# Output projection with the first norm, and experts with the second norm, each as one stage worked tile by tile; rank matmuls 256 columns wide

## The reference, cut to what matters

```
o   = y @ out_proj.T                     # 1024 x 1024 by 1024 x 512
x   = x + layernorm(o)
h   = layernorm(x)
low = h @ A.T ; g = gates(h @ W_gate.T, h @ W_thr)      # 8 experts of rank 16
o   = h @ W_base.T + b_base + (2 * low * g) @ B
x   = x + layernorm(o)
h   = rmsnorm(layernorm(x)) * norm_w     # goes into layer 1
```

## Time and profile before

| | us |
|---|---|
| median of 3 runs | 2665.6 |
| lowest, highest | 2663.9, 2677.38 |
| span of the profiled execution | 2670.2 |
| TensorE busy in it | 2308.2 (86%) |
| VectorE busy | 1957.9 (73%) |
| ScalarE busy | 1460.8 (55%) |
| GpSimd busy | 1238.2 (46%) |

### The profile page before, as it was taken

How to read it: one execution, slowest core, us unless ns; L and a number is a source line. 1 busy time by engine, 2 the same in 40 slices (tenths; PEclk the granted TensorE clock), 3 DMA queues, 4 the chain that set the end, 5 groups by cost and what they waited for, 6 DMA issues and landing times. The chain is left out here.

```text
span 2670.2 us, 33973 instructions
## 1 busy us (share of the span) xinstructions
PE 2308.2 (86%) x11172; PEld 1672.4 (63%) x11172; DVE 1957.9 (73%) x3153; ACT 1460.8 (55%) x3092; POOL 1238.2 (46%) x788
## 2 busy tenths in 40 slices
PE   5966676667454999999999999999999999779997
PEld 4532222225434677777777777777777777569996
DVE  4559989994554786686685776775866866688777
ACT  2344444443103796685785866866956857742221
POOL 2119988993101464363462553644643624542212
PEclk9989998998576999999999999999999999899999
DMA  2030030000112232231332322322312312211010
GB/s 80 26 115 13 0 126 0 0 0 32 60 36 74 90 119 66 76 115 52 90 99 57 101 76 71 111 72 74 108 67 77 113 52 88 91 45 37 36 48 32
DMA packets 113218, 175.20 MB, mean 66 GB/s; under 512 B 9696, under 2 KB 77664, under 8 KB 112032
## 3 DMA queue, kind: packets, MB, share of 16 engines
q1 hardware_dynamic: 113056, 173.16, 20.6%
HBM read 166.71 MB, written 6.42 MB: 65 GB/s over the span
## 5 line engine op out<-in xcount | busy, mean ns | idle before, releaser
L78 PE MATMUL mg_pb<-xTh,mg_wh 128*128 128x512 f32 x1152 | 479.2, 416 | 16.9 <-POOL mg_wl L1233 16.9
L1243 POOL TENSOR_TENSOR mg_y<-mg_hT,mg_sg 128x512 f32<-128x512 f32 x128 | 187.7, 1466 | 598.9 <-DVE mg_hT L1479 598.9
L79 PE MATMUL mg_pb<-xTl,mg_wh 128*128 128x512 f32 x1152 | 454.3, 394 | 0.0
L80 PE MATMUL mg_pb<-xTh,mg_wl 128*128 128x512 f32 x1152 | 452.1, 392 | 0.0
L775 PE MATMUL ss_y<-ss_pr,cst 128*128 128x512 f32 x512 | 278.5, 678 | 125.7 <-POOL ss_pr L757 125.4
L1427 DVE SCALAR_TENSOR_TENSOR mg_hT<-mg_pb,mg_cw,mg_hT 128x510 f32<-128x510 f32 (+2 forms) x432 | 318.4, 741 | 31.6 <-ACT mg_hT L1599 22.8
L757 POOL TENSOR_TENSOR ss_pr<-o,ss_bc 128x1024 f32<-128x1024 f32 x128 | 301.9, 2374 | 45.9 <-DVE o L726 26.9
L1454 DVE TENSOR_TENSOR mg_m<-mg_gb,mg_cb 128x384 f32<-128x384 f32 x512 | 265.3, 549 | 71.6 <-ACT mg_gb L1649 68.2
L775 PEld LDWEIGHTS ss_y<-ss_pr,cst 128*128 128x128 f32 x512 | 98.4, 210 | 305.6 <-POOL ss_pr L757 225.8
L657 ACT ACTIVATE ss_da<-dt,ss_na 128x510 f32 (+1 forms) x256 | 165.9, 680 | 208.0 <-DVE o L726 208.0
L78 PEld LDWEIGHTS mg_pb<-xTh,mg_wh 128*128 128x128 f32 x1152 | 217.2, 189 | 76.5 <-issue 19.2
(11 more groups left out here) (289 smaller groups left out, 5217.4 us busy)
## 6 DMA issues: line engine op xcount, KB each, us to landing
mg_abc<-acs_rows SPq DMA_DIRECT2D x256, 256.0 KB, 3.4
mg_ws<-in_w_in SPq DMA_DIRECT2D x72, 512.0 KB, 3.8
ss_bc<-bc_rows SPq DMA_DIRECT2D x16, 1024.0 KB, 6.4
mg_wos<-in_w_out SPq DMA_DIRECT2D x64, 256.0 KB, 3.6
ff_ws<-in_w SPq DMA_DIRECT2D x7, 1024.0 KB, 4.7
x<-in_x SPq DMA_DIRECT2D x16, 256.0 KB, 4.1
ip_ws<-in_w_in SPq DMA_DIRECT2D x8, 512.0 KB, 3.6
ff_w2s<-in_w SPq DMA_DIRECT2D x7, 512.0 KB, 5.7
```

Source lines behind the costliest of these rows:

```text
L78: pe.matmul(out, lhs[0], rhs[0], start=start, stop=False)
L79: pe.matmul(out, lhs[0], rhs[1], start=False, stop=False)
L80: return pe.matmul(out, lhs[1], rhs[0], start=False, stop=stop)
L1243: pool.tensor_tensor(yb[:, p % RING, t], hT[s % 2][:, t], sg[s % 2][:, t], ALU.mult).then_inc(s_y2, 1)
```

## The change

Both norm stages are taken apart. The first norm of all (`first_norm`) keeps its operations. `out_proj_and_norm` takes the place of `scan_out_proj` and the n1 norm, `experts_and_norm` that of `experts` and the n2 norm. The 1024 channels' weights come in four transfers of two k-tiles into two buffers; x and the expert weights are loaded behind the first two. The projection runs tiles 0 to 3 with k outermost in four pairs of k, and tiles 4 to 7 one by one. As soon as a tile is done, its statistics, norm, addition and second norm follow per tile; GpSimd adds x, ScalarE norms o straight from its bank. In the experts stage the split of the weights is made at its start by ScalarE, VectorE and GpSimd; the rank matmuls read 256 columns (the last 118 of the base weights and the 138), of which the last 138 are used; the second scaling uses the variance instead of a sum of squares (var * r * r), norm_w is multiplied in by GpSimd before the transposition, and x_kept is written by tile. Semaphores of finished stages are cleared by SyncE and used again.

```diff
+def out_proj_and_norm(nc, sem, clear_stages, spare, sb, banks, I, xc, sz, o, x, xT, ex_ws, cst, eps, x_tok):
...
+            def _(sp):
+                for j in range(HT):
+                    if j >= 2:
+                        sp.wait_ge(s_wl, j - 1)
+                    sp.dma_start(ws[j % 2][:], I["w_out0"][:, 2 * j:2 * j + 2, :]).then_inc(s_w[j % 2], 16)
+                    if j == 1:
+                        for m in range(MT):
+                            sp.dma_start(x[:, m, :], x_tok[:, m, :]).then_inc(s_x, 16)
+                        sp.dma_start(ex_ws[:], I["w_ex"]).then_inc(s_x, 16)
+                cleared.extend(clear_stages(sp, "ip_", "sp_", "ss_", "n0_", "norm_"))
+                sp.wait_ge(s_x, 16 * (MT + 1))
...
+                def low(j):
+                    pool.wait_ge(s_hi, j + 1)
+                    wait_buffer(pool, j)
+                    pool.tensor_tensor(held(yl[j % 2], j), part(xc, j), held(yh[j % 2], j).bitcast(F32), ALU.subtract
+                                       ).then_inc(s_lop, 1)
+
+                def add_x(m):
+                    pool.wait_ge(s_n1, m + 1)
+                    pool.tensor_tensor(x[:, m, :], x[:, m, :], o[:, m, :], ALU.add).then_inc(s_x2, 1)
+
+                for j in range(HT):
+                    weights_low(j)
+                low(4)
+                pool.wait_ge(s_x, 16 * (MT + 1))
+                low(5)
+                for m in range(MT):
+                    add_x(m)
+                    if m < 2:
+                        low(6 + m)
...
+                for j in range(HT):
+                    pair(j)
+                tile(4)
+                tile(5)
+                turn(0)
+                turn(1)
+                tile(6)
+                turn(2)
+                turn(3)
+                tile(7)
+                for m in range(4, MT):
+                    turn(m)
...
+                high(4)
                 for m in range(MT):
...
+                    root(0, m)
+                    if m >= 1:
+                        root(1, m - 1)
+                    norm_o(m)
+                    if m < 3:
+                        high(5 + m)
+                    if m >= 2:
+                        x_high(m - 2)
...
+                for m in range(MT):
+                    stats_o(m)
+                    if m >= 1:
+                        stats_x(m - 1)
+                    invert_o(m)
+                    if m < 2:
+                        gated(6 + m)
+                    if m >= 1:
+                        normed(m - 1)
+                    if m >= 2:
+                        x_low(m - 2)
...
+def experts_and_norm(nc, sem, clear_stages, spare, sb, banks, I, xT, x, o, ex_ws, st_w, cst, eps, x_dram):
...
+                for m in range(MT):
+                    add_x(m)
+                    if m >= 1:
+                        weighted(m - 1)
+                weighted(MT - 1)
...
+                def rank(m):
+                    if m >= 2:
+                        pe.wait_ge(s_g, m - 1)
+                    t = slice(m * P, (m + 1) * P)
+                    for k in range(KD):
+                        i = mm3(pe, pk[m % 2][:, 0:RW], (xT[0][:, k, t], xT[1][:, k, t]),
+                                (wh[:, k, DM + N2 - RW:], wl[:, k, DM + N2 - RW:]), k == 0, k == KD - 1)
+                    i.then_inc(s_p, 1)
...
+                pe.wait_ge(s_wlv, 2)
+                pe.wait_ge(s_wlp, 2)
+                for m in range(MT):
+                    rank(m)
                 for m in range(4):
...
+                    base(m)
+                pe.wait_ge(s_b, 64)
+                turn_hw(0)
                 for m in range(MT):
...
+                    if m + 1 < MT:
+                        turn_hw(m + 1)
+                    up(m)
+                    if m + 4 < MT:
+                        base(m + 4)
+                    if m >= 3:
+                        turn(m - 3)
+                for m in range(MT - 3, MT):
+                    turn(m)
...
+                for k in range(KD):
+                    act.activation(wh[:, k, :], ex_ws[:, k, :], ACT.Copy).then_inc(s_wh, 1)
...
+                for m in range(MT + 3):
+                    if m < MT:
+                        copied(m)
+                        root(0, mv[0][:, m, 1:2], m)
+                    if 1 <= m <= MT:
+                        root(1, mv[1][:, m - 1, 1:2], m - 1)
+                    if m < MT:
+                        norm_o(m)
+                    if 1 <= m <= MT:
+                        root(2, ms[:, m - 1:m], m - 1)
+                    if 2 <= m <= MT + 1:
+                        scaled(m - 2)
+                    if m >= 3:
+                        x_high(m - 3)
...
+                for m in range(MT + 3):
+                    if m < MT:
+                        biased(m)
+                    if 1 <= m <= MT:
+                        stats_x(m - 1)
+                    if m < MT:
+                        invert_o(m)
+                    if 1 <= m <= MT:
+                        normed(m - 1)
+                        second(m - 1)
+                    if m >= 3:
+                        x_low(m - 3)
...
             @block.tensor
             def _(pe):
-                pe.wait_ge(s_lo, 2 * KD)
                 for h in range(NH):
```

More of the change, by code:

```diff
@@ new lines, in tile, with turn @@
+                def tile(m):
+                    pe.wait_ge(s_lop, m - HT + 1)
+                    if m >= 6:
+                        pe.wait_ge(s_n1, m - 5)
+                    hi, lo = held(yh[m % 2], m), held(yl[m % 2], m)
+                    for k in range(CD):
+                        last = mm3(pe, bank(m)[:], (hi[:, k, :], lo[:, k, :]), (wh[:, k, :], wl[:, k, :]),
+                                   k == 0, k == CD - 1)
+                    last.then_inc(s_out, 1)
+                def turn(m):
+                    pe.wait_ge(s_h, m + 1)
+                    if m >= 2:
+                        pe.wait_ge(s_xlo, m - 1)
+                    for k in range(KD):
+                        last = pe.transpose(tb[m % 2][:, k * P:(k + 1) * P], o[:, m, k * P:(k + 1) * P], ident)
+                    last.then_inc(s_t, 1)
@@ L853, in experts, with gated, low @@
-def experts(nc, sem, sb, banks, I, xT, o, ident, weights):
+                ch = Chain(dve, s_ch)
+                def gated(j):
+                    dve.wait_ge(s_sz, j + 1)
+                    dve.tensor_tensor(part(xc, j), part(xc, j), part(sz, j), ALU.mult).then_inc(s_y, 1)
+                def low(j):
+                    dve.wait_ge(s_hi, j + 1)
+                    wait_buffer(dve, j)
+                    dve.tensor_tensor(held(yl[j % 2], j), part(xc, j), held(yh[j % 2], j).bitcast(F32), ALU.subtract
+                                      ).then_inc(s_lo, 1)
@@ new lines, in _ @@
+                gated(0)
+                gated(1)
+                for j in range(HT):
+                    low(j)
+                    gated(j + 2)
+                for m in range(MT):
+                    stats_o(m)
[8 more added lines that the diff above has]
+                        x_low(m - 2)
@@ new lines, in _ @@
+                for m in range(MT):
+                    copied(m)
+                gates()
+                dve.wait_ge(s_b, 64)
+                for m in range(MT + 3):
[10 more added lines that the diff above has]
+                        x_low(m - 3)
@@ L969, in ring_runs @@
+        spare.extend(cleared)
 def ring_runs(g):
@@ L979, in mixer_steps @@
     with ExitStack() as c:
-        _, _, wh, wl, _ = weights
-        s_lo = sem("early_w_lo")
+        _, wh, wl = weights
         db = sb(c, "st_db", [P, 1])
```

671 lines of the change are left out of this document (361 added, 310 removed).

## The result

The changed kernel takes 2636.42 us (median of 4 runs, 2634.85 to 2640.62) where the kernel before takes 2668.84 (4 runs beside it, 2663.90 to 2677.38): a ratio of 0.9868, interval 0.9850 to 0.9887. Faster by 32 us; forecast were 43, to 2623, in a range of 2610 to 2641. Direction and range held, the size was a third too large. The profiled execution of after took 2640.62, with a span of 2638.8. Executions over 1.5% above the fastest of their kernel are left out of every median; there were two, both of one kernel (3891.85 and 7483.42 us).

What follows compares the result with a forecast made beforehand. TensorE and VectorE were taken to bound alternate stages, none overlapping, over 201.3 us. Gains of 27.8 (first edit) and 15.3 (second), 43.1 us, off the median 2665.6 gave 2622.5, rounded 2623; range 2610 to 2641.

Steps and rivals of the forecast that it cites:

- Start of TensorE: Projection stage: first matmul at 621.0, 4.9 us earlier, since weights come in four pieces.
- The third weight piece: Projection stage: lands about 628, needed split by 634, covered by 1 to 2 us; if late, TensorE waits as much.
- Rounds of the first stage: Joined projection and norm: GpSimd queues low parts and adds behind ScalarE's norm and high part, 6.8 us a round.
- rival (a): Rank projection: wide matmuls stay at 0.50, 20.5 us instead of 12.9, base starts low, 2.9 more: 2633; 12%.
- The gates: Experts stage: 6.6 us, ending at 714.9, hidden beside the base projection; without that cover they would show in full.
- Shift 0: Second stage: first tile's shift at 724.0, after up matmul, bias, statistics, table load and root.
- The share of the wide rank matmuls: Second stage: widening 138 columns to 256 gives 7.1 us of that edit's 15.3.
- the time from shift 0 to shift 7: Second stage: rounds of 3.4 and 3.9, then five of 5.5 us with GpSimd weighting before adding; 724.0 to 758.8.
- base 4 to 7 and the up matmuls: Second stage: they need about 4.2 us of TensorE a round and stay under the round's length.
- (c): Both stages: TensorE loses its clock at waits before tiles 6 and 7 and in second-stage rounds, 17 us: 2640; 13%.
- (b): VectorE, not GpSimd's order, sets second-stage rounds, 4.6 not 5.5; first-stage rounds nearer 5.5 than 6.8: 2615; 15%.
- (d): Both stages: VectorE and GpSimd block each other, 16 tiles lose 58 us: 2681, 2%; half 2652, 3%; quarter 2638, 5%.

Runs made afterwards that it cites:

- the filler: Changed kernel plus twenty idle 256-column matmuls after the turn in each of four late experts-stage rounds: 2635.73 us, ratio 0.9870.
- first stage alone: Changed kernel with only the joined projection and first norm; experts and second norm as before, 138 rank columns: 2650.89 us, ratio 0.9923.
- the last kernel: Up matmul queued ahead of base matmuls, added to the kernel with copy ahead, add first, high part early, low parts on VectorE: 2614.82 us.

## Why the prediction was right or wrong

**Right by its own steps.** Start of TensorE: forecast 8.3 us into the stage, was 8.8. The third weight piece, the risk named, was split at 633.56 and held nobody. Rounds of the first stage 6.8, were 6.65. End of the projection 66.3 into the stage, was 64.2, the tail 10.2, was 10.8: together 1.5 better. Split of the expert weights 5.9, was 5.5. Rank projection 12.9, was 13.0, with a low-clock start of 3.2 us instead of 3.8; rival (a) fell. The gates stayed hidden beside the base (the first weighting is at 718.69, the base ends behind it). Shift 0: 34.8 into the stage, was 33.8. Tail behind shift 7: 12.1, was 12.4. The steps stage (27.9) and the rest (1827.8) kept their lengths. The share of the wide rank matmuls was put at 7.1 and is 9.1, because a rank projection at 1.00 also hands its clock to the base (rival (a) had counted that, the share had not); the sum had both lengths right and only that share wrong.

**The step that failed** is one term, the time from shift 0 to shift 7: 3.4 + 3.9 + 5 x 5.5 = 34.8 forecast, 43.5 measured. These 8.7, with the 1.0 that the stage was ahead at shift 0 and 0.3 in the tail, are the 8.0 by which the second stage is longer than worked out. It has three causes.

The first two rounds are 2.9 us too long: "base 4 to 7 and the up matmuls need about 4.2 us a round of TensorE and stay under it" compared sums of busy time. The up matmul's place in the queue, behind base matmuls that wait for the bias, makes it a loop of 5.1 (4.8 in the kernels with the early copy), and the kernel with the up matmul ahead, 3.45 and 3.8, shows it gone.

The other five rounds are 5.8 us too long: the order I followed was norm, root, scaling on ScalarE and weighting, add on GpSimd, and I left ScalarE's last item, the copy for the next up matmul, out of the circle; the kernel with the copy ahead has 27.1 us for these five where after has 33.3.

And of each of the three 7.1 us rounds 0.9 is the low clock, some 2.7 of the 5.8; the filler shows it for the last two. The low clock counts only because the up matmul stands in that circle: with the copy ahead two up matmuls still take 1.92, and the rounds are 5.43.

One of the forecast's own signs had failed with it: shifts 5.5 us apart with GpSimd's add waited for. The result, 2636, lies near (c)'s 2640, but not for its reason: (c) took the lost clock of the base matmuls for the whole of the loss, and these never lost it; the orders were about 6.0 of the 8.7. That the time stayed in the range is luck in part: the range reached to 2641 to take in (c), and this term had no room of its own in it.

**The other rivals.** (b) supposed VectorE as the setter of the rounds. In after it was not, at 7.1 us; it took the changes of order to make it so. (d), VectorE and GpSimd in each other's way, set no round of the second stage: there VectorE's passes of 512 columns, which read a matmul's bank or have one input, take 0.54 to 0.69, also in the kernel with rounds of 4.4 us, with GpSimd busy 7.53 of 13 us beside it. But the two do get in each other's way at the start of the first stage. A pass of GpSimd in after, and the second and the last of VectorE's four low parts:

```profile
627.44 3.04 POOL L736 TENSOR_TENSOR op_wl<-op_ws,op_wh 128x1024 fp32r<-128x1024 f32 x1 [1.44 <-ACT op_wh L814]
628.34 3.22 DVE L868 TENSOR_TENSOR op_yl<-xc,op_yh 128x1024 fp32r<-128x1024 f32 x1
...
641.43 1.25 DVE L868 TENSOR_TENSOR op_yl<-xc,op_yh 128x1024 fp32r<-128x1024 f32 x1 [2.10 <-ACT op_yh L819]
```

The three that run beside GpSimd take 2.52 to 3.22 us, the one that does not 1.25. The first of the three is what TensorE's start waits for; behind it TensorE does not stop before turn 1, so the others cost nothing that the trace shows.

What stays open: why the first stage was 1.5 us shorter than forecast. The difference is there at its first shift, 31.9 us into the stage (650.28) where 33.8 was forecast, within its estimates. Open is also how short the second stage would be were TensorE's clock kept up throughout, and what the up matmul ahead would give without the other changes of order.

## What to carry to other kernels

Working tile by tile across four engines pays only as far as the order on each engine lets it: go once round the circle from a tile's step to the same step of the next tile, through every queue, and write down each item that stands between, also the one at the very end of the round. Sums of busy time per engine (4.2 of TensorE, 4.6 of VectorE) made 5.5 us a round look safe. In the second stage four changes of order, each of a few lines, were worth more (89.7 to 72.4 us) than working it tile by tile in the first place (102.8 to 98.8). What the next tile needs from an engine goes to the head of its round, what only the far end needs goes last.

## What was not expected of the hardware

A matmul of 138 columns took as long as one of 256 at the low level (0.213 us), and 20.5 us of them without a gap left the grant at 0.50, while 256-column ones, in the same place, were at 1.00 after 3.2 us. Here the widening cost nothing and the clock rose; it gained 9.1 and 9.2 us by windows in two kernels.

The same pause can cost the clock or not. In the front part TensorE pauses 0.96 us ahead of a short matmul pair. This code is the same in both kernels, only its line numbers differ. First the timeline of the kernel before, then that of after:

```profile
108.81 1.04 PE L436 MATMUL sp_pq<-sp_sq,cst 64*64 64x512 f32 x2 [0.96 <-ACT sp_sq L557]
109.78 0.50 PE L78 MATMUL ip_pb<-xTh,ip_wh 128*128 128x512 f32 x1
110.11 0.40 PE L79 MATMUL ip_pb<-xTl,ip_wh 128*128 128x512 f32 x1
```

```profile
110.41 1.04 PE L328 MATMUL sp_pq<-sp_sq,cst 64*64 64x512 f32 x2 [0.96 <-ACT sp_sq L449]
111.38 0.60 PE L78 MATMUL ip_pb<-xTh,ip_wh 128*128 128x512 f32 x1
111.78 0.63 PE L79 MATMUL ip_pb<-xTl,ip_wh 128*128 128x512 f32 x1
112.20 0.63 PE L80 MATMUL ip_pb<-xTh,ip_wl 128*128 128x512 f32 x1
```

Matmuls 0.23 us apart there, 0.43 us apart here for some 3.5 us, and once more from 121.9 to 125.3 us. After was 1.6 us behind already at the pause. Of the 13 kernels' profiles five (after, before with wide rank matmuls, low parts on VectorE, first stage alone, high part early) have a grant of 0.80 from 110 to 127 us, the last kernel has 0.90, the other seven 1.00. In the eleven kernels with the new first stage its first matmul is at 623.7 to 627.2 us in the four of them with 0.80, and at 620.6 to 622.8 in the other seven. What decides it no run here shows, nor that the grant accounts for all of the difference. It limits what a median of this kernel can tell: two versions that differ by under 5 us are told apart by the windows of their stages.
